# A fused attention, scan and expert layer: who splits the keys when, and who does the last sums, norms and constants

## The reference

```python
x = x + xattn(layernorm(x), ctx, ctx, w_proj, b_proj)     # 16 heads of 32, ctx is [4, 2048, 512], keys = values
x = x + scan_block(layernorm(x))
x = x + experts(layernorm(x))                             # 8 experts, top 2, and two shared ones

def scan_block(x):                                        # x is already the normed row here, and its residual too
    xn = x * rsqrt(mean(x * x) + 1e-8) * norm_w
    u, z, g = split(xn @ W_in + b_in, 3)
    ut, dt = tanh(u @ W_x + b_x), sigmoid(z @ W_dt + b_dt)
    h = scan(h * (1 - dt) + dt * ut)
    return x + (h * sigmoid(g)) @ W_out + b_out
```

## Time and profile before

| | us |
|---|---|
| median of 3 runs | 535.68 |
| lowest and highest | 532.35, 535.93 |
| the profiled execution's own time | 537.27 |
| its span | 535.5 |

### The profile page before, as it was taken

How to read it: one execution, slowest core, us unless ns; L and a number is a source line. 1 busy time by engine, 2 the same in 40 slices (tenths; PEclk the granted TensorE clock), 3 DMA queues, 4 the chain that set the end, 5 groups by cost and what they waited for, 6 DMA issues and landing times.

```text
span 535.5 us, 15785 instructions
## 1 busy us (share of the span) xinstructions
PE 468.8 (88%) x6731; PEld 329.2 (61%) x6731; DVE 401.7 (75%) x598; ACT 329.7 (62%) x362; POOL 290.4 (54%) x274
## 2 busy tenths in 40 slices
PE   0468887999999999999989955999999999999994
PEld 0126555676666766667666532844878788787642
DVE  3467665787877788787771799698599999999426
ACT  3327465776767777776654373456579888788320
POOL 2045698899999999999769430482001101010042
PEclk9999898999999999999999996999999999999998
DMA  7986799878888987987992731076999999997125
GB/s 201 239 194 202 194 257 273 241 206 223 248 255 251 265 255 188 256 223 183 359 375 97 295 97 61 1 253 232 416 355 412 416 420 416 417 417 319 40 85 171
DMA packets 48253, 133.97 MB, mean 250 GB/s; under 512 B 6452, under 2 KB 31284, under 8 KB 37428
## 3 DMA queue, kind: packets, MB, share of 16 engines
q1 hardware_dynamic: 43928, 120.38, 69.3%
q0 software_dynamic: 3680, 12.06, 6.2%
q10 hardware_dynamic: 576, 0.52, 0.5%
HBM read 96.77 MB, written 11.01 MB: 201 GB/s over the span
## 4 chain that ended last, share of the span: by engine, by line
PE 45%; DVE 34%; DMA 8%; issue 8%; ACT 2%; POOL 2%; SPq 1%; DVEq 0%; ACTq 0%; POOLq 0%
DVE mx L720 11%; DVE ws L805 9%; PE bank L1059 8%; PE bank L1024 8%; PE bank L1068 6%; PE bank L1044 6%; DMA wst<-in_ffw 5%; PE bank L1186 2%; PE bank L1188 2%; DVE rden L737 2%; PE bank L1187 2%; DMA kstk<-kl 2%; DVE hf L946 1%; PE bank L1129 1%; DVE hl L951 1%
## 5 line engine op out<-in xcount | busy, mean ns | idle before, releaser
L720 DVE TENSOR_REDUCE mx<-bank 128x1 f32<-128x512 f32 x240 | 152.7, 686 | 60.2 <-PE bank L1024 60.0
L475 ACT ACTIVATE pt<-bank 128x1024 f32<-128x1024 f32 x128 | 126.0, 1023 | 70.8 <-PE bank L1044 69.5
L636 POOL TENSOR_TENSOR ps<-pt 128x512 f32<-128x512 f32 x128 | 159.8, 1275 | 14.8 <-PE bank L1068 9.2
L805 DVE SCALAR_TENSOR_TENSOR ws<-wst,ws 128x2048 f16<-128x2048 f32 x51 | 115.6, 2286 | 2.6 <-ACT ws L523 2.4
L523 ACT ACTIVATE ws<-wst 128x2048 f16<-128x2048 f32 x48 | 90.5, 1904 | 5.9 <-DMA wst<-in_ffw 5.7
L611 POOL TENSOR_TENSOR kl<-kt,kh 128x512 f16<-128x512 f32 x58 | 67.4, 1185 | 27.4 <-ACT kh L440 27.4
L1201 PE MATMUL bank<-xt,ws 128*128 128x128 f16 x480 | 81.2, 219 | 1.1 <-DVE hf L946 1.1
L1202 PE MATMUL bank<-xt,ws 128*128 128x128 f16 x480 | 81.2, 219 | 0.0
L1203 PE MATMUL bank<-xt,ws 128*128 128x128 f16 x480 | 81.2, 219 | 0.0
L1024 PE MATMUL bank<-kstk,q 96*128 96x512 f16 x176 | 66.6, 420 | 15.6 <-DMA kstk<-kl 7.5
L677 POOL DMA_DIRECT2D ys_rows<-xn x15 | 8.1, 543 | 121.7 <-ACT xn L592 121.7
(11 more groups left out here) (170 smaller groups left out, 719.0 us busy)
## 6 DMA issues: line engine op xcount, KB each, us to landing
wst<-in_ffw SPq DMA_DIRECT2D x51, 1024.0 KB, 11.0
kt<-in_keysT SPq DMA_DIRECT2D x16, 1024.0 KB, 6.3
v<-in_vals SPq DMA_DIRECT2D x16, 1024.0 KB, 9.7
kstk<-kh SPq DMA_DIRECT2D x84, 128.0 KB, 3.3
kstk<-kl SPq DMA_DIRECT2D x44, 128.0 KB, 2.8
wst<-kh SPq DMA_DIRECT2D x40, 128.0 KB, 2.8
xs_rows<-biases SPq DMA_DIRECT2D x15, 256.0 KB, 3.0
x_tok<-xs_rows POOLq DMA_DIRECT2D x15, 256.0 KB, 8.5
```

The source lines that it names most:

```text
L475: act.activation(pt[:, n % 4, :, :, :].rearrange("p j a t -> p (j a t)"), bank[:, 2 * (n % 2):2 * (n % 2) + 2, :].rearrange("p j n -> p (j ...
L636: pool.tensor_tensor(ps2[:, n % 4, :, :], pt[:, n % 4, 0, :, :], pt[:, n % 4, 1, :, :], ALU.add)\
L720: dve.tensor_reduce(mx[:, a, q:q + 1], bank[:, 4 + k % 2, :], AX.X, ALU.max).then_inc(m_taken, 1)
L805: dve.scalar_tensor_tensor(ws[:, home_of(q), 1, m, :, :].rearrange("p c n -> p (c n)"), wst[:, q % 2, m, :, :].rearrange("p c n -> p (c n) ...
```

## The change

Three things.

1. **Key splits and loads.** Group 0 is now like all others. ScalarE splits the keys of group i + 3 in double steps 2 and 3, the first one behind `take_shifted`; GpSimd splits them after pair sums 5 and 7. VectorE splits group 0's keys alone (2 x 128x1024), GpSimd those of groups 1 and 2 ahead of its first pair sum. ScalarE's queue issues no copies. SP loads x's rest and the second keys before the first copies, issues the copies of group 0 half by half, and has the V load between the two halves of a stack.
2. **Ends of the attention.** The pair sums of group 15 are VectorE's. Bias sums stand after pair sums 2 and 5 of groups 13 and 14. The constants' loads are spread over groups 4 to 7, the first expert's weights over groups 8 to 10; `split_first(0)` is in group 14. `scale_win` and the experts' constants stand between VectorE's pair sums of group 15; `split_low(0, 0)` comes before the projection's first add.
3. **Normed row and residual.** The normed row xn is no longer written. VectorE forms two factors per row and x2 = x1 * (1 + r) - m * r in one operation, GpSimd adds b_out to it. A sigmoid of two elements loads ScalarE's table ahead of dt.

```diff
@@ SP
         def load_k(j):
             if j >= 2:
-                sp.wait_ge(split_lo, j - 1)
-                sp.wait_ge(lo_dve, 2 * min(j // 2, 2))
+                sp.wait_ge(split_lo, j - 2)
+            if j == 2:
+                sp.wait_ge(lo_dve, 2)
...
         load_k(0)
         sp.dma_start(idh[:, :], t["idh"]).then_inc(id_in, 16)
+        sp.dma_start(x[:, 1:B, :], t["x"][:, 1:B, :]).then_inc(x_in, 16)
+        load_k(1)
+        stack(0, 0)
+        stack(0, 1)
         sp.dma_start(kstk[KS:KM, :, :, :], t["ones"]).then_inc(ones_in, 16)
         sp.dma_start(stacks[2][KS:KM, :, :], t["ones"][:, 0, :, :]).then_inc(ones_in, 16)
...
             if i + 3 < G:
                 stack(i + 3, 0)
+            if i + 2 < G:
+                load_v(i + 2)
+            if i + 3 < G:
                 stack(i + 3, 1)
...
+            for dst, name in CONSTS[3 * i - 12:3 * i - 9] if 4 <= i < 8 else []:
+                sp.dma_start(dst, t[name]).then_inc(consts, 16)
+            if 8 <= i < 11:
+                sp.dma_start(wst[:, 0, i - 8, :, :], t["ffw"][0, i - 8]).then_inc(w_in[0][i - 8], 16)
@@ ScalarE
                 for n in scores_in(i, p):
                     exponent(n)
+                if i == G - 2 and p == 1:
+                    split_first(0)
                 if p == 1 and i + 2 < G:
                     take_queries(i + 2)
-                if i == 0 and p < 2:
-                    split_keys(2, p)
-                if p in ((2, 3) if i == 0 else (0, 1)) and i + 3 < G:
-                    split_keys(i + 3, p % 2)
                 if p == 2 and i + 1 < G:
                     take_shifted(i + 1)
+                if p >= 2 and i + 3 < G:
+                    split_keys(i + 3, p - 2)
                 if p == 3 and i + 3 < G:
                     queries_high(i + 3)
@@ GpSimd
-        for i in range(G):
+        for i in range(G - 1):
             for hs in range(HS):
                 pair_sum(HS * i + hs)
-                if i == 0 and hs == 4:
-                    split_keys(2, HG - 1)
-                if hs in ((5, 7) if i == 0 else (3, 5)) and i + 3 < G:
-                    for a in ((0, 1) if hs == (5 if i == 0 else 3) else (2, 3)):
+                if hs in (5, 7) and i + 3 < G:
+                    for a in range(hs - 5, hs - 3):
                         split_keys(i + 3, a)
                 if hs == HS - 1 and i + 3 < G:
                     queries_low(i + 3)
-        add_bias()
+                if i in (G - 3, G - 2) and hs in (2, 5):
+                    add_bias(2 * (i - G + 3) + hs // 3)
...
-            pool.wait_ge(x1_done, b + 1)
-            pool.tensor_tensor(x2[:, b, :], x1[:, b, :], bout[:, :], ALU.add).then_inc(x1b_done, 1)
-        for b in range(B):
-            pool.wait_ge(h_done, b + 1)
-            pool.wait_ge(x1b_done, b + 1)
-            pool.tensor_tensor(x2[:, b, :], x2[:, b, :], xn[:, b, :], ALU.add).then_inc(x2p_done, 1)
+            pool.wait_ge(x1h_done, b + 1)
+            pool.tensor_tensor(x2[:, b, :], x2[:, b, :], bout[:, :], ALU.add).then_inc(x2p_done, 1)
@@ VectorE
         for i in range(G):
-            if i == G - 1:
-                scale_win()
             for p in range(HS // 2):
                 for j, k in maxima_in(i, p):
                     take_max(j, k)
+                if i == G - 1:
+                    for n in (HS * i + 2 * p, HS * i + 2 * p + 1):
+                        pair_sum(n)
...
+                if i == G - 1 and p == 0:
+                    scale_win()
+                if i == G - 1 and p == 1:
+                    make_constants()
...
             dve.tensor_scalar(hn[:, b, :], x1[:, b, :], mv[:, b, 0:1], lnv[:, 3, b:b + 1], ALU.subtract, ALU.mult)\
                 .then_inc(hn_done, 1)
-            dve.tensor_scalar(xn[:, b, :], x1[:, b, :], mv[:, b, 0:1], lnv[:, 2, b:b + 1], ALU.subtract, ALU.mult)\
-                .then_inc(h_done, 1)
+            link(dve.scalar_tensor_tensor(r1[:, 1, b:b + 1], mv[:, b, 0:1], -1.0, lnv[:, 2, b:b + 1], ALU.mult, ALU.mult))
+            dve.tensor_scalar(r1[:, 2, b:b + 1], lnv[:, 2, b:b + 1], 1.0, None, ALU.add).then_inc(rows_made, 1)
+            dve.wait_ge(rows_made, b + 1)
+            dve.tensor_scalar(x2[:, b, :], x1[:, b, :], r1[:, 2, b:b + 1], r1[:, 1, b:b + 1], ALU.mult, ALU.add)\
+                .then_inc(x1h_done, 1)
```

More of the change, by code:

```diff
@@ L343, in copies @@
         def copies(j, h, src, rows):
-            stack_rows(sp, j, h, src, rows)
+            for row in rows:
+                for q in (2 * h, 2 * h + 1):
+                    sp.dma_start(stacks[j % 3][row:row + HD, :, q * S // 4:(q + 1) * S // 4],
+                                 src[q * HD:(q + 1) * HD, j % 2, :, :]).then_inc(k_rep[j % 3][h], 16)
         def stack(j, h):
@@ L492, in _ @@
         for h in range(2):
-            split_keys(1, h)
+            split_keys(2, h)
         take_shifted(0)
```

126 lines of the change are left out of this document (55 added, 71 removed).

## The result

The changed kernel took 542.07 us (median of 6, 540.04 to 544.66), the kernel before 535.8 beside it: ratio 1.012, 95% interval 1.008 to 1.016. It is 1.2% slower, where 534.0 was forecast with 522 to 541 as the range. The profiled run has a span of 542.5 for 535.5, and the two traces split these 7.0 us as follows.

A forecast was written before the change was run, and what follows sets the result against it. TensorE, hand in hand with VectorE's maxima, was taken to set the period of 15.19, with GpSimd nearly full. Opening -6.8, even groups +8.3, last groups +0.4 and norm to scan -3.5 sum to -1.6: 534.0, range 522 to 541.

The forecast's parts named there:

- First maxima -5.8: Opening: VectorE's first maxima at 15.9 for 21.76, 5.8 earlier.
- Scores at 28.3: Opening: scores start at 28.3, where they started at 34.13; the 12.4 from first maxima to scores stay.
- this cover thin: Opening: third keys split by 27, just ahead of ScalarE's next copy, wanted at 27.5.
- S(1): Moment at which TensorE starts the four shift transposes of group 1; forecast at 45.4 for 52.20, 6.8 earlier.
- Of its 2.10 some 1.0 held the maxima: Opening, group 0: VectorE no longer makes its key split of 2.10, which brings S(1) forward by 1.0.
- The loop, 16.7 a group: Even groups: ScalarE's split after the shift copy and GpSimd's before sums 6 and 7 make 16.7 for 15.19; +8.3.
- All covered: Even groups: V, keys, constants and first weights, the last two loaded in groups 4 to 10, all come when wanted.
- Last groups +0.4: Attention's last groups and projection: one late denominator costs 0.4; at the projection nothing gained or lost.
- Norm to scan -3.5: From the norm to scan_b: 3.5 less, as VectorE is free earlier and ScalarE decides; bounds -1.5 and -4.5.
- A (no loop): Rival, even groups: the loop does not bind, 19.5 less, 514.5; chance 0.16.
- B (clock): Rival, even groups: TensorE's new stops lower its clock, 2 a group more, 560; chance 0.10.
- C: Rival, opening: copies stuck behind the loads, only 1.0 gained, S(1) at 51.2, 540; chance 0.10.

The follow-up runs named there:

- the relieved kernel: The changed kernel with both engines' key splits back, V load first, constants and weights in groups 12 and 13, bias sums from group 14 on: 526.0, ratio 0.980.

## Why the prediction was wrong

- **First maxima -5.8: right** (-6.2). **Scores at 28.3: wrong** (32.08). The step that failed is "the third keys are issued at 18, land at 25 and are split by 27". They landed at 29.4: I gave a 1 MB load 7 us, while twelve copies of the second keys and the first V were issued within 9 us behind it. I had called this cover thin and kept no case for it. Behind it lay a second wait that I had not looked for at all: the second keys' copies. Taking the first away alone won 1.0 of the missing 4.7 at S(1) (and 0.7 in the relieved kernel; both within what single traces vary), taking both away 3.8.
- **What a load costs the copies behind it: asked of the wrong transfers.** The first keys' copies were in time (the last awaited one landed at 15.46, 15.9 forecast). The first half of the second keys' copies, behind the third load, landed at 25.4 to 33.7 in after, and at 22.0 to 26.7 with the load moved behind them. In its own sentence: the Trainium skill (DMA: Bandwidth & Descriptors, Queues, rings and completion order) has descriptors consumed in ring order on each engine. What I drew from it, that no copy moves before the loads in front, the trace does not bear out as it stands: the first copy behind the third load landed 4.1 before that load did. The copies behind a load are slower (6.7 to 11.7 for 3.3 and 2.8), but they are not held until it has landed.
- **"Of its 2.10 some 1.0 held the maxima": right, and cancelled.** In the kernel before, TensorE stood 1.11 for VectorE's maxima behind that split, and after has no such stop:

```profile
49.98 0.39 PE L1024 MATMUL bank<-kstk,q 96*128 96x512 f16 x1 [1.11 <-DVE mx L720]
```

Yet from scores to S(1) pass 18.07 before and 18.00 after. In both kernels the products run at the lower clock level's pace until about 43 (8 score products take 1.06, later 0.61), and after starts its scores 2.1 earlier, so more of its work falls into that time: its first 32 value products take 1.94 for 1.44. I had not thought of the clock here. With the opening's loads moved as well, the stretch is 17.41.
- **The loop, 16.7 a group: right** (16.55), in each of its pieces: 2.08 for 2.17 to GpSimd's start, 9.85 for 9.82 plus hand-over to the denominators, 4.62 for 4.65 after. Its term is 13 x 16.54 - 208.75 = +6.3 for +8.3.
- **"All covered": wrong, and the costliest.** This is the second step that failed. Constants and weights beside a DMA share of 0.84 gave four groups 5.7 more: two stops for late instructions (groups 7 and 8) and two for late copies (12 and 13); 0.84 was a mean, and V between the copies alone had already raised the keys' landing from 5.8 to 8.2 (the two kernels with the loop closed and the loads late). I priced the loads by bytes, 2.5 each, and asked whether each was there in time. The runs show that the price is paid by others: copies behind the loads, and TensorE's instructions.
- **Last groups +0.4: 1.15 measured.** The scaling and the constants cost what was forecast; not forecast was a stop of 1.5 before the last sums. It is an instruction stop (at 298.73, instruction 34 x 256 + 193), while weights loaded and the zero rows were stored. Where bias sums stood behind group 14 and the zero rows came later, that stop is missing and S(15) to the projection took 13.6 to 13.7 for 14.8, in seven versions.
- **Norm to scan -3.5: right** (-4.25, inside the bounds): 0.6 by the joint row, 1.6 by the constants and weights in the last group (1.1 net, as they cost 0.5 ahead of the projection), from the runs that undo them; the other 2.0 were not taken apart.
- **Rivals.** A (no loop): fell at 16.55. B (clock): fell, the windows have 1.00 over the first five groups with all the stops of 0.3; in the even part the clock fell only behind the stops of 1.59 and 1.79, not behind those of 1.36 and 1.48. C, copies stuck behind loads, was asked of the first maxima and fell there; copies slowed behind a load were at work 15 us later.
- The sum: opening 4.7 too good, loop 2.0 too dear, stops 5.7 left out, last groups 0.75 short, norm 0.75 too little, tail 0.2: 4.7 - 2.0 + 5.7 + 0.75 - 0.75 + 0.2 = 8.6, which with -1.6 makes the 7.0 measured.

Shown by runs: the loop and its place, the loads' and V's share, the opening's two waits. Shown by the traces: that TensorE waits for its instructions at the stops in the middle of value products, and for copies or V at the others that are named above. Not shown: why an instruction packet comes late. Of the 42 instruction stops 38 stand in the seven versions with V between the copies all through, and the version with V first and the same loads has only one, though its DMA share over 120 to 240 us is as high (1.01 for 0.99 in after); no run isolates what in V's place makes the difference. The same loads cost four groups 5.7 in the one profiled run of after and two 2.8 with the shift copy first, so their number is partly chance.

## What to carry to other kernels

Before moving work off the critical path, walk the loop that the new order closes, piece by piece from rows: that number came out within 1%. But opening such a loop pays only as far as the next limit, here the transfers: opening it won nothing (544.1 for 542.1) with V and the extra loads in the way, and 20.8 us (526.0 for 546.8, 8.0 of them in the last group but one) without them. Price an added transfer by what stands behind it in its queue, not by its bytes or its own due time, and in an opening follow every transfer issued behind a large load to who waits for it. And where a profile says "issue", look for the landing just before: of data here in one kind of stop, of the engine's own instructions in the other.

## What was not expected of the hardware

- A mean DMA share of 0.84 to 0.88 was the clean state and 1.01 to 1.08 the stopped one in after and with the splits back; with equal bytes a group, V's place alone moved the keys' landing from 5.7 to 9.7.
- TensorE stops for up to 2.3 in the middle of products that wait for no data: its instructions come in packets of 16 KB, one for every 256 of them, through the DMA engines that carry the data, and can be late. The DMA share of the 10 us before the 42 stops was 0.92 to 1.11.
- After a stop of 3.7 a group takes 8.1 longer: the products behind it take 1.93 for 1.06.
